# Masked attention with layer norm on one core: ScalarE copies each block's weighted sums out of PSUM, and VectorE's finish moves behind the mask operation

## The reference

```python
scores = jnp.einsum('nd,md->nm', x, ks)              # x, ks: 8192 x 128, f32
scores = jax.nn.leaky_relu(scores, negative_slope=0.2)
scores = jnp.where(adj > 0, scores, -9e15)           # adj: 8192 x 8192, int32, 0 or 1
attn = jax.nn.softmax(scores, axis=1)
x = layernorm(x + jnp.einsum('nm,md->nd', attn, ks)) # over the last axis, eps 1e-5
```

## Time and profile before

| | before |
|---|---|
| median of 3 runs | 1573.85 us (1573.39 to 1574.77) |
| profiled execution, own time | 1574.71 us |
| its span in the profile | 1572.5 us |
| mean granted TensorE clock | 0.996 of full speed |
| TensorE busy (weight loads) | 1505.3 us, 96% (1418.3 us, 90%) |
| VectorE busy | 1508.1 us, 96% |
| ScalarE busy | 1466.0 us, 93% |
| GpSimd busy | 1437.6 us, 91% |
| mean DMA rate | 188 GB/s |

### The profile page before, as it was taken

How to read it: one execution, slowest core, us unless ns; L and a number is a source line. 1 busy time by engine, 2 the same in 40 slices (tenths; PEclk the granted TensorE clock), 3 DMA queues, 4 the chain that set the end, 5 groups by cost and what they waited for, 6 DMA issues and landing times.

```text
span 1572.5 us, 42991 instructions
## 1 busy us (share of the span) xinstructions
PE 1505.3 (96%) x16832; PEld 1418.3 (90%) x16832; DVE 1508.1 (96%) x1788; ACT 1466.0 (93%) x1810; POOL 1437.6 (91%) x1237
## 2 busy tenths in 40 slices
PE   1689999999999999999999999999999999999997
PEld 1479999999999999999999999999999999999996
DVE  6899999999999999999999999999999999999983
ACT  4489999999999999999999999999999999999997
POOL 1789999999999999999999999999999999999998
PEclk9999999999999999999999999999999999999999
DMA  9755555455555555555555555545555555555520
GB/s 357 261 202 180 185 198 198 166 197 196 192 181 197 187 197 179 194 198 193 181 186 199 183 188 199 196 166 198 197 188 185 197 186 196 181 195 196 190 70 8
DMA packets 67530, 296.38 MB, mean 188 GB/s; under 512 B 6400, under 2 KB 32512, under 8 KB 34560
## 3 DMA queue, kind: packets, MB, share of 16 engines
q1 hardware_dynamic: 67328, 293.63, 53.2%
HBM read 289.41 MB, written 4.19 MB: 187 GB/s over the span
## 4 chain that ended last, share of the span: by engine, by line
PE 74%; ACT 11%; issue 8%; DVE 3%; POOL 2%; DMA 1%; SPq 1%; ACTq 0%; DVEq 0%; POOLq 0%
PE weighted L652 20%; PE scores L618 11%; PE scores L620 11%; PE scores L619 11%; PE weighted L668 7%; PE weighted L664 6%; PE weighted L666 6%; ACT ring L403 5%; ACT pt_hi L410 4%; DVE running L540 1%; DMA ring<-in_x_t 1%; ACT xt_hi L378 1%; PE floors L637 1%; POOL pt_lo L323 1%; POOL ring L318 1%
## 5 line engine op out<-in xcount | busy, mean ns | idle before, releaser
L318 POOL TENSOR_TENSOR ring<-ring,floor 128x512 f32<-128x512 f32 (+2 forms) x512 | 713.1, 1393 | 64.9 <-ACT floor L421 64.9
L323 POOL TENSOR_TENSOR pt_lo<-ring,pt_hi 128x512 f16<-128x512 f32 (+1 forms) x512 | 658.6, 1287 | 14.5 <-ACT pt_hi L410 11.4
L525 DVE SCALAR_TENSOR_TENSOR ring<-adj_sb,scores 128x1024 f32<-128x1024 int32 x512 | 620.7, 1212 | 12.1 <-ACT scores L397 7.4
L397 ACT ACTIVATE scores<-scores,shrink 128x1024 f32<-128x1024 f32 x512 | 554.2, 1082 | 74.5 <-PE scores L620 69.4
L618 PE MATMUL scores<-xt_hi,kt_hi 128*128 128x256 f16 x2048 | 559.8, 273 | 51.7 <-DVE xt_lo L490 29.4
L403 ACT ACTIVATE ring<-ring,lift 128x1024 f32<-128x1024 f32 x512 | 582.7, 1138 | 1.6 <-POOL ring L318 1.6
L620 PE MATMUL scores<-xt_hi,kt_lo 128*128 128x256 f16 x2048 | 560.2, 274 | 0.0
L619 PE MATMUL scores<-xt_lo,kt_hi 128*128 128x256 f16 x2048 | 559.9, 273 | 0.0
L540 DVE TENSOR_TENSOR running<-ring,running 128x1024 f32<-128x1024 f32 x448 | 547.2, 1222 | 0.1
L652 PE MATMUL weighted<-k_rows,ring 128*128 128x129 f32 x3584 | 488.0, 276 | 2.1 <-DVE y L577 1.3
L652 PEld LDWEIGHTS weighted<-k_rows,ring 128*128 128x128 f32 x3584 | 440.8, 192 | 14.4 <-ACT ring L403 9.8
(11 more groups left out here) (54 smaller groups left out, 433.6 us busy)
## 6 DMA issues: line engine op xcount, KB each, us to landing
adj_sb<-in_adj SPq DMA_DIRECT2D x256, 1024.0 KB, 4.8
ring<-in_ks_t SPq DMA_DIRECT2D x8, 512.0 KB, 6.5
ring<-in_x_t SPq DMA_DIRECT2D x8, 512.0 KB, 12.6
xt_raw<-in_x_t SPq DMA_DIRECT2D x32, 128.0 KB, 5.0
x_row<-in_x SPq DMA_DIRECT2D x32, 128.0 KB, 5.8
out<-normed SPq DMA_DIRECT2D x32, 128.0 KB, 5.1
k_rows<-in_ks SPq DMA_DIRECT2D x12, 128.0 KB, 3.1
ring<-in_ks SPq DMA_DIRECT2D x12, 128.0 KB, 3.0
```

Source lines behind the costliest of these rows:

```text
L318: nc.gpsimd.tensor_tensor(here, here, below, ALU.subtract).then_inc(gap_ready, 1)
L323: nc.gpsimd.tensor_tensor(pt_lo[:, g % PARTS, 0:QUAD - whole, :], ring[:, g % RING, whole:, :], pt_hi[:, g % PARTS, 0:QUAD - whole, :], AL ...
L525: nc.vector.scalar_tensor_tensor(ring[:, g % RING, :, :], adj_sb[:, n % ADJS, half * QUAD:(half + 1) * QUAD, :], 0.0, scores[:, g % 2, :, ...
```

## The change

ScalarE gets a new step, `sums_of`, in the finish slot, between `high_part` and `exponentials`. It waits until the block's last group is weighed and copies the 258 columns of `weighted` to a new SBUF tile, `sums`. VectorE's `finish` waits for this copy and reads it in place of the PSUM tile; in VectorE's loop it now stands behind `mask`. TensorE's first `weigh` of the next block waits for the copy and no longer for `y`. The program reserves 4096 bytes for dynamic DMA descriptors in place of the default.

```diff
+        sums = sb("sums", [P, SIDES, LANES], F32)
+        sums_ready = sem("sums_ready")
...
+            def sums_of(b):
+                act.wait_ge(weighted_ready, GROUPS * (b + 1))
+                wait(act, y_ready, SIDES * b)
+                nc.scalar.activation(sums.rearrange("p j w -> p (j w)"), weighted[:, 0:SIDES * LANES], ACT.Copy)\
+                    .then_inc(sums_ready, 1)
...
                 if g is not None:
                     high_part(g)
+                b = whole(s, AT_FINISH)
+                if b is not None:
+                    sums_of(b)
                 g = group(s, AT_EXP)
                 if g is not None:
                     exponentials(g)
...
             def finish(b):
                 at = b % 2
-                total = weighted[:, 0:SIDES * LANES].rearrange("p (j w) -> p j w", j=SIDES)
-                dve.wait_ge(weighted_ready, GROUPS * (b + 1))
-                nc.vector.tensor_scalar(denom[:, :], total[:, :, ONES], scale_k, None, ALU.mult).then_inc(denom_ready, 1)
+                dve.wait_ge(sums_ready, b + 1)
+                nc.vector.tensor_scalar(denom[:, :], sums[:, :, ONES], scale_k, None, ALU.mult).then_inc(denom_ready, 1)
...
-                    nc.vector.scalar_tensor_tensor(y[:, j, :], total[:, j, 0:D], recip[:, j:j + 1],
+                    nc.vector.scalar_tensor_tensor(y[:, j, :], sums[:, j, 0:D], recip[:, j:j + 1],
...
             for s in SLOTS:
-                b = whole(s, AT_FINISH)
-                if b is not None:
-                    finish(b)
                 g = group(s, 0)
                 if g is not None:
                     mask(g)
+                b = whole(s, AT_FINISH)
+                if b is not None:
+                    finish(b)
...
                 if q == 0:
-                    wait(pe, y_ready, SIDES * b)
+                    wait(pe, sums_ready, b)
...
-    nc = bacc.Bacc("TRN2", target_bir_lowering=False, num_devices=1)
+    nc = bacc.Bacc("TRN2", target_bir_lowering=False, num_devices=1, dynamic_dma_scratch_size=4096)
```

More of the change, by code:

```diff
@@ L581, in _ @@
             for s in SLOTS:
+                g = group(s, 0)
+                if g is not None:
+                    mask(g)
                 b = whole(s, AT_FINISH)
@@ L584, in _ @@
                     finish(b)
-                g = group(s, 0)
-                if g is not None:
-                    mask(g)
                 b = whole(s, AT_LOWEST)
```

## The result

The changed kernel takes 1652.49 us (median of 4 runs, 1651.31 to 1653.07) against 1573.73 before (median of 4 runs): a ratio of 1.0496, 95% interval 1.0484 to 1.0509. It is 78.8 us slower; the forecast was 58.2 us slower, 1632 us, with a range up to 1645. The sign and the place were right and the size was not. The profiled execution took 1651.31 us, its span is 1649.1 us, 76.6 more than before.

What follows compares the result with a forecast made beforehand. TensorE and VectorE, both busy practically throughout, were taken to bound the kernel, neither able to make up a stall. Blocks 56.5, emptying 1.4 and end 0.3 sum to +58.2 us: 1632 us, range 1618 to 1645.

Steps and rivals of the forecast that it cites:

- (d): The block's loop: VectorE busy from mask to column minimum, TensorE stalling; 48.57 us against 46.70, +1.87 per block.
- (b): ScalarE's queue, finish slot: the copy stands still 2.3 us, delaying `bend`; the mask starts 2.42 us after the copy.
- (c): VectorE's finish, moved behind the mask and reading SBUF: 0.91 us in place of 1.07, bounds 0.77 and 1.07.
- (a): TensorE's wait for `y` before the next block's first `weigh` goes: alone gives back 0.26 us per block.
- (g): The rest, including later GpSimd `mean` and ScalarE squares, SyncE's wait and the smaller reserve: costs nothing.
- (e): How often the block loss occurs: 30 finish slots x 1.87 = 56.1 us, plus 0.4 at the last `turn`.
- (f): The emptying: GpSimd is 1.4 us later behind ScalarE's `high_part`, and the very end adds 0.3 us.
- TensorE's loop sets the block: Rival: stalls at slot 9 and `turn` don't come; +0.78 us per block, 1599 us; chance 0.09.
- The clock falls: Rival: TensorE's pauses lower its clock once per block; 52 us more, 1684 us; chance 0.04.
- Faster: Rival: ScalarE's wait hurts nobody, the finish slot's mask starts by 793.48; 8 us less, 1566 us; chance 0.03.

Runs made afterwards that it cites:

- e2: The changed kernel with the copy moved behind `bend` in ScalarE's queue: 1592.0 us, ratio 1.0112.
- e10: The changed kernel with GpSimd's `mean` moved ahead of `low_part`, so that GpSimd runs nothing during finish: 1641.2 us, ratio 1.0422.
- e11: The changed kernel with the copy behind `bend` and GpSimd's `mean` moved into the finish slot behind `split_x`: 1601.5 us, ratio 1.0172.
- e6: The kernel before with only the smaller reserve for dynamic DMA descriptors: 1574.1 us, ratio 1.0000.
- e1: The changed kernel with `denom` written as a tensor_tensor multiplication, the scale as second SBUF source: 1652.9 us, ratio 1.0496.
- e7: The changed kernel with the copy behind `bend` and finish ahead of the mask: 1625.4 us, ratio 1.0327.
- the probes: Six small VectorE operations per block, SBUF to SBUF, read by nobody, added to the kernel before with the smaller reserve: 1672.2 us, one run.

## Why the prediction was wrong in size and right in mechanism

The loop of step (d), as forecast and as the changed kernel's trace has it:

| | forecast | measured |
|---|---|---|
| mask to the end of the column minimum | 32.32 | 862.48 - 829.57 = 32.91 |
| handoff and turn to copy | 13.83 | 827.14 - 813.25 = 13.89 |
| copy to mask | 2.42 | 2.43 |
| block | 48.57 | 49.23 |

- **(b) ScalarE's wait: right.** 2.33 us idle in each block, and `bend` and the mask behind it where they were forecast. e2 removes this and three quarters of the loss; it is by far the larger cause.
- **(c) the length of finish: this is the step that failed.** I took 0.91 us and gave 1.07 as the upper bound; it is 1.49. Of the 0.58 us, 0.16 is a saving that doesn't exist (e10: 1.07 from SBUF as from PSUM), and 0.42 is the hold by GpSimd's `low_part`, which the sum put at nothing. With the 0.07 of the other two lines it is 0.66 per block, 20 us in 30 blocks. 58 + 20 is 78, where the medians differ by 78.8 and the profiled executions by 76.6. Two faults led to it. I compared two different operations, `denom` and the reciprocal, to price the memory that they read, when the second is simply the shorter one. The fixed cycles that the Trainium skill gives (page "VectorE: DVE Perf Modes", section on the TRN2 errata) would by estimate have made it 0.19; here the measurement decides, and it is nothing: `denom` takes 0.22 us from PSUM and, with GpSimd idle, 0.22 from SBUF (e10, e11), and `y` 0.35 from both. And I asked what an operation costs in SBUF without asking who else uses SBUF then. The trace before could not show a hold at that place, since finish read PSUM there. But it shows one at another place, which I overlooked: the first `least` of a block, whose two inputs are both in SBUF, takes 1.22 to 1.23 us in 31 blocks, where no GpSimd operation runs when it starts, and 2.11 in the first block, where one does:

```profile
39.40 2.11 DVE L540 TENSOR_TENSOR running<-ring 128x1024 f32<-128x1024 f32 x1
```

```profile
37.20 2.13 POOL L284 TENSOR_TENSOR kt_lo<-ring,kt_hi 128x1024 f16<-128x1024 f32 x1
39.31 1.12 POOL L280 TENSOR_SCALAR ring<-ring,scale 128x1024 f32<-128x1024 f32 x1
40.52 2.98 POOL L284 TENSOR_TENSOR kt_lo<-ring,kt_hi 128x1024 f16<-128x1024 f32 x1
```

It ends 1.08 us behind the GpSimd operation that ran at its start (41.51 against 40.43), which is about its own length. GpSimd's `kt_lo` took 2.13 us before and takes 2.98 beside it. Both directions of the hold were on record.
- **(d) the stalls: right.** TensorE waits 0.86 and 1.02 us at the scores of slots 8 and 9 and 0.29 at `turn` (1.0, 0.6 and 0.4 forecast); the second is 0.4 larger than forecast because finish is longer. VectorE has no gap between the mask and the minimum.
- **(a), (g): right.** TensorE no longer waits for `y`, and the reserve costs nothing (e6).
- **(e) the count: right**, 30 x 2.54 = 76.2 us of the span's 76.6.
- **(f) the emptying: too dear.** 1.7 us was forecast. From the last column minimum to the end it is 49.60 us before and 50.21 after, 0.6 more; but the two differ in the clock too. In the changed kernel TensorE paused 2.91 us for the last minimum, and the clock stayed:

```profile
1598.00:1600.00 2.00, 0.00 (x0) 1.00 0.00 0
1600.00:1604.00 4.00, 3.85 (x49) 1.00 0.01 4
```

In the kernel before, 2.36 us of pause were followed by a stretch at 0.57. The traces of e6, which is the kernel before but for the reserve, and of e1, where the column minimum and its pause (2.90 us) are those of the changed kernel, have it the other way round:

```profile
1524.00:1528.00 4.00, 4.00 (x52) 1.00 0.02 4
```

```profile
1600.00:1604.00 4.00, 3.46 (x25) 0.50 0.00 0
```

So a pause of this length is sometimes followed by the lower clock, and sometimes not. From the last minimum to the end e6 takes 49.06 us and e1 52.53. Between the two without the lower clock, e6 and the changed kernel, the emptying is 1.1 us longer. The stretch that the prediction priced at 1.72 us cost 0.5 there (before against e6), and the longer one of e1 about 2.3 (against the changed kernel). That the profiled execution of the changed kernel was the fastest of the four fits this: its mean granted clock is 0.997, that of the others 0.995 to 0.996, with spans 1.1 to 1.7 us longer. They were not traced.

The rivals: *TensorE's loop sets the block* did not happen, since the stalls at slot 9 and `turn` came. *The clock falls* did not happen either: it is 1.00 from 60 to 1640 us, with three pauses of up to 1.02 us in every block. *Faster* needed a mask by 793.48 on the scale of the block before, and with 2.43 us from copy to mask it came 1.0 us too late, as forecast; e2 shows that even with the mask in time the copy loses to GpSimd's hold. The range was too narrow because its upper end held only the term's price from PSUM.

## What to carry to other kernels

Before a step with a wait goes into an in-order queue, look at what stands behind it there and how soon that is needed: one move of the copy, from ahead of `bend` to behind it, was worth 60 us of 79. When an operand moves from PSUM to SBUF, look at what GpSimd runs at that time: an operation with nothing but SBUF operands can be held until GpSimd's operation ends, so a task of 0.2 us may take 0.6 or 1.2. A timeline of the kernel before can already show such a hold elsewhere: the same operation, long where GpSimd is busy and short where it is idle. And where two engines are both full, work removed from the step that both wait for (here `denom`, 0.25 us a block) gives more than work moved to a third engine.

## What was not expected of the hardware

`tensor_scalar` with its tensor in SBUF, and `tensor_tensor` and `scalar_tensor_tensor` with two SBUF tensors, are held to the end of a running GpSimd operation: `denom` takes 0.63 us in the changed kernel and 1.13 on the mean in e7, the probes 1.12 and 0.86, `y` 0.94 and once 1.34, all operations that take 0.16 to 0.35 us by themselves. A small operation is not spared: two elements per partition are held like 128. The reciprocal (0.15 to 0.16 us in all 59 probes) is not. The hold can be seen in the trace only in the duration: no wait is listed for it. GpSimd is lengthened in turn: from 1.83 to 2.10 us in e11, from 2.13 to 2.98 in the kernel before. A pause of TensorE of 2.4 or 2.9 us before the emptying was followed by the lower clock in one trace and not in another of the same or nearly the same kernel.
